# Output projection of a cross-attention block: one float32 product against three float32r products of high and low parts

## What is computed

```python
attn = attn.reshape(b, n, N_HEADS * HEAD_DIM)
return attn @ Wout + bout
...
x = x + _L0_xattn_ref(_layernorm(x, axis=-1), ctx_1024, ...)
x = x + _L0_ffn_ref(_layernorm(x, axis=-1), L0_ffn_w_fc, L0_ffn_w_proj)
```

## Time and profile before

| | us |
|---|---|
| median of 3 runs | 822.95 |
| lowest and highest run | 822.5, 823.52 |
| the profiled execution, its own time | 822.28 |
| its span in the trace | 820.2 |
| PE busy | 778.4 |
| DVE busy | 682.1 |
| ACT busy | 451.8 |
| POOL busy | 337.5 |

### The profile page before, as it was taken

How to read it: one execution, slowest core, us unless ns; L and a number is a source line. 1 busy time by engine, 2 the same in 40 slices (tenths; PEclk the granted TensorE clock), 3 DMA queues, 4 the chain that set the end, 5 groups by cost and what they waited for, 6 DMA issues and landing times.

```text
span 820.2 us, 11697 instructions
## 1 busy us (share of the span) xinstructions
PE 778.4 (95%) x3842; PEld 331.7 (40%) x3842; DVE 682.1 (83%) x937; ACT 451.8 (55%) x825; POOL 337.5 (41%) x428
## 2 busy tenths in 40 slices
PE   1899989799999999999999999899999999999996
PEld 0688877132222222222222222234444444444442
DVE  5988876978888888888888888369999999988983
ACT  4566666177777777777777777744322432233230
POOL 2777867654345544554455545323221211111000
PEclk9999999599999999999999999999999999999998
DMA  8278887734455566675556663226456645553463
GB/s 275 91 204 229 260 231 182 168 92 137 124 140 157 144 138 155 143 162 162 141 150 176 172 162 102 65 61 142 103 116 145 126 90 110 111 127 78 79 127 90
DMA packets 175627, 116.14 MB, mean 142 GB/s; under 512 B 116560, under 2 KB 147280, under 8 KB 175568
## 3 DMA queue, kind: packets, MB, share of 16 engines
q1 hardware_dynamic: 175568, 115.40, 57.6%
HBM read 64.50 MB, written 25.43 MB: 110 GB/s over the span
## 4 chain that ended last, share of the span: by engine, by line
PE 82%; DVE 7%; DMA 3%; ACT 3%; issue 2%; SPq 1%; POOL 1%; DVEq 0%; ACTq 0%; POOLq 0%
PE banks L638 15%; PE banks L625 15%; PE banks L599 13%; PE banks L871 11%; PE banks L883 10%; PE banks L256 8%; PE banks L857 7%; PE banks L280 1%; DVE h_scales L951 1%; DMA stack_words<-max_rows 1%; DVE maxima L669 1%; DVE h_stats L938 1%; ACT probs_words L689 1%; ACT probs_words L1001 1%; DMA probs_words<-in_L_xattn_Wkv_dram 1%
## 5 line engine op out<-in xcount | busy, mean ns | idle before, releaser
L669 DVE TENSOR_REDUCE maxima<-banks 128x2 f32<-128x1024 f32 x256 | 301.8, 1216 | 50.2 <-PE banks L599 50.2
L689 ACT ACTIVATE probs_words<-banks 128x512 f32<-128x512 f32 x512 | 276.0, 597 | 99.9 <-PE banks L625 98.2
L625 PE MATMUL banks<-stack_words 98*128 98x512 bf16 x512 | 175.0, 385 | 2.9 <-ACT probs_words L689 1.8
L599 PE MATMUL banks<-stack_words 96*128 96x512 bf16 x512 | 158.9, 392 | 5.2 <-DVE maxima L669 4.6
L638 PE MATMUL banks<-probs_words,late_words 128*32 128x512 f32 x1024 | 136.4, 605 | 0.5
L883 PE MATMUL banks<-ternary_words,stack_words 128*128 128x512 f16 x512 | 115.3, 384 | 4.5 <-DMA stack_words<-stack_words 4.5
L871 PE MATMUL banks<-ternary_words,late_words 128*128 128x512 f16 x512 | 113.1, 379 | 0.0
L1001 ACT ACTIVATE probs_words<-probs_words,h_moments 128x2048 f32<-128x2048 f32 x16 | 32.0, 2002 | 136.8 <-DVE h_moments L943 136.8
L625 PEld LDWEIGHTS banks<-stack_words 98*128 98x128 bf16 x512 | 39.4, 97 | 143.6 <-ACT probs_words L689 85.1
L703 POOL TENSOR_SCALAR neg_max<-maxima 128x16 f32<-128x16 f32 x32 | 8.3, 258 | 173.4 <-DVE maxima L669 173.4
L883 PEld LDWEIGHTS banks<-ternary_words,stack_words 128*128 128x128 f16 x512 | 50.6, 99 | 70.6 <-issue 14.3
(11 more groups left out here) (127 smaller groups left out, 935.4 us busy)
## 6 DMA issues: line engine op xcount, KB each, us to landing
o_rows<-late_words SPq DMA_DIRECT2D x32, 256.0 KB, 2.7
k_parts<-ternary_words SPq DMA_DIRECT2D x48, 128.0 KB, 2.9
q_parts<-ternary_words SPq DMA_DIRECT2D x48, 128.0 KB, 2.5
stack_words<-q_parts SPq DMA_DIRECT2D x32, 192.0 KB, 3.0
stack_words<-k_parts SPq DMA_DIRECT2D x96, 64.0 KB, 2.7
stack_words<-k_parts SPq DMA_DIRECT2D x32, 192.0 KB, 2.8
attn_words<-in_x_dram SPq DMA_DIRECT2D x16, 256.0 KB, 4.4
probs_words<-in_L_ffn_w_fc_dram SPq DMA_DIRECT2D x16, 256.0 KB, 4.1
```

The source lines that it names most:

```text
L599: mm = self.nc.tensor.matmul(self.score_slot[j % 2][:, i], self.mem.q_stack[0:STACK, slot, head, c * P:(c + 1) * P], self.mem.k_stack[0:ST ...
L625: self.nc.tensor.matmul(self.mem.banks[:, self.ST_BANK[k]], self.mem.k_stack[0:STACK + 2, slot, head, c * P:(c + 1) * P], self.mem.q_stack ...
L669: dve.tensor_reduce(self.maxima[:, g % 2, 2 * j:2 * j + 2], self.score_slot[j % 2], AX.X, ALU.max).then_inc(self.scores_read, 1)
L689: act.activation(self.probs[:, c, head, :], self.mem.banks[:, self.ST_BANK[k]], ACT.Exp, scale=1 / math.sqrt(HEAD)).then_inc(self.exp_done, 1)
```

## The change

`Wout` and each tile of `attnT` are split into a high part, rounded to float32r, and a low part, the rest. `mix` then issues 12 float32r matmuls (high by high, attention high by weight low, attention low by weight high) in place of 4 float32 ones. The new work around it:

- DVE: `weight_high` (two copies of 128x1024) and `weight_low` (two subtractions of 128x1024), once, around the copy of the sums of group 29.
- ACT: `mix_high`, one copy of 128x512 for each of the 16 tiles: for tiles 0 and 1 inside the exponentials of two late attention steps, for tile 2 right after the first `centre_u`, for tile 3 after the second, for later ones after the `centre_u` of their iteration.
- POOL: `mix_low`, one subtraction of 128x512 for each tile: for tiles 0 and 1 in the last attention steps, for tile 2 after `spread_u` of tile 1, for tile 3 after `add_bias` of tile 3, for later ones straight after `add_bias` of the same tile.
- `mix` of tile n now waits for `mix_low` of tile n.
- The parts have memory of their own under v; raw `Wout` is loaded into a slot of the attention stacks, at a later place of SP's queue, x into the buffers of the raw ternary weights, and some other buffers move.

```diff
--- before.py
+++ after.py
@@ -84,6 +84,11 @@
         self.gammas = sb("gammas", [P, 2], F32)
         self.limits = sb("limits", [P, 2, 2], F32)
         self.half_power = sb("half_power", [P, 1], F32)
+        with ExitStack() as early:
+            self.wout_parts = [early.enter_context(nc.sbuf_tensor(f"wout_{part}", [P, KX, DIM], F32R))[:]
+                               for part in ("high", "low")]
+            self.mixT = [early.enter_context(nc.sbuf_tensor(f"mixT_{part}", [P, 2, KX, P], F32R))[:]
+                         for part in ("high", "low")]
         self.v_words = sb("v_words", [P, GROUPS * CHUNKS * GW], F32)
         self.v_all = self.v_words[:].rearrange("p (g c e) -> p g c e", c=CHUNKS, e=GW)
         with ExitStack() as early:
@@ -467,9 +472,9 @@
         self.inverse = slots(late.take(2 * SEQ), 2)
         self.v_ones = late.take(2 * CHUNKS * GH * 2 * HEAD).rearrange("p (s c h e) -> p s c h e", s=2, c=CHUNKS, h=GH)
         self.raw = slots(late.take(2 * DIM), 2)
-        self.below = late.take(DIM // 2, F16)
         self.ternary = slots(late.take(DIM, F16), 2)
         self.late = late
+        self.below = mem.late_words[:, 22 * DIM - DIM // 2:22 * DIM].bitcast(F16)
         self.sums = sb("sums", [P, 2, SUMS], F32)
         self.maxima = sb("maxima", [P, 2, GH * CHUNKS], F32)
         self.neg_max = sb("neg_max", [P, 2, GH * CHUNKS], F32)
@@ -741,17 +746,19 @@
         self.nc, self.mem, self.att = nc, mem, att
         sb, late, banks = mem.sb, att.late, mem.banks
         blocks = lambda words, n: words.rearrange("p (k d) -> p k d", k=n)
-        self.x1 = [late.take(DIM) for i in range(X1_SLOTS - 1)]
+        self.x1 = [late.take(DIM) for i in range(X1_SLOTS - 1)] + [att.ternary.rearrange("p s c -> p (s c)").bitcast(F32)]
         self.u_parts = late.take(2 * DIM, F16).rearrange("p (s t c) -> p s t c", s=2, t=2)
         self.uT = late.take(U_SLOTS * DIM, F16).rearrange("p (s i r) -> p s i r", s=U_SLOTS, r=P)
+        self.bout_sb = late.take(DIM)
+        self.u = mem.late_words[:, 21 * DIM:22 * DIM]
+        self.x_in = att.raw
+        self.wout_raw = [mem.stack_words[:, i * half:i * half + 2 * DIM].rearrange("p (k d) -> p k d", k=2)
+                         for half in (STACK_SLOTS * GH * SEQ // 2,) for i in range(2)]
+        self.wout_parts, self.mixT = mem.wout_parts, mem.mixT
         values = Region(mem.v_words)
-        self.wout_sb = blocks(values.take(KX * DIM), KX)
-        self.bout_sb = values.take(DIM)
-        self.x_in = blocks(values.take(2 * DIM), 2)
+        values.take((KX + 2) * 2 * DIM)
         self.centred = blocks(values.take(2 * DIM), 2)
-        self.u = values.take(DIM)
         self.y = blocks(values.take(2 * DIM), 2)
-        self.x1.append(values.take(DIM))
         self.h = mem.probs_words[:].rearrange("p (s c) -> p s c", s=H_SLOTS)
         stacks = Region(mem.stack_words)
         self.h_parts = stacks.take(2 * FFN, F16).rearrange("p (s t c) -> p s t c", s=2, t=2)
@@ -778,6 +785,10 @@
         self.h_turned = [[sem(f"h_turned_{slot}_{part}") for part in range(2)] for slot in range(2)]
         self.out_stored = [sem(f"out_stored_{i}") for i in range(2)]
         self.wout_loaded = sem("rows_wout_loaded")
+        self.wout_high = sem("rows_wout_high")
+        self.wout_low = sem("rows_wout_low")
+        self.mixT_high = sem("rows_mixT_high")
+        self.mixT_low = sem("rows_mixT_low")
         self.bout_loaded = sem("rows_bout_loaded")
         self.x_bias_ready = sem("rows_x_bias_ready")
         self.mix_ready = sem("rows_mix_ready")
@@ -810,15 +821,16 @@
 
 
     def load_bias(self, sp, bout):
-        sp.wait_ge(self.att.v_staged, 3 * HG)
         sp.dma_start(self.bout_sb, bout.rearrange("(a d) -> a d", a=1).to_broadcast([P, DIM])
                      ).then_inc(self.bout_loaded, DMA)
 
     def load_weight(self, sp, wout, k):
-        sp.wait_ge(self.att.v_staged, 3 * HG)
-        sp.dma_start(self.wout_sb[:, k], wout[k * P:(k + 1) * P]).then_inc(self.wout_loaded, DMA)
+        sp.wait_ge(self.att.st_ready, (GROUPS - STACK_SLOTS + 1) * 16)
+        sp.dma_start(self.wout_raw[k // 2][:, k % 2], wout[k * P:(k + 1) * P]).then_inc(self.wout_loaded, DMA)
 
     def load_x(self, sp, x, n):
+        if n < 2:
+            sp.wait_ge(self.att.ternary_ready, GROUPS - 1 + n)
         need(sp, self.x1_ready, n - 1)
         sp.dma_start(self.x_in[:, n % 2], x.rearrange("b (c p) d -> (b c) p d", p=P)[n]
                      ).then_inc(self.x_in_loaded[n % 2], DMA)
@@ -846,16 +858,15 @@
 
 
     def mix(self, pe, n):
-        att = self.att
-        pe.wait_ge(att.divided, (n // CHUNKS + 1) * KX)
+        pe.wait_ge(self.mixT_low, n + 1)
         if n == 0:
-            pe.wait_ge(self.wout_loaded, KX * DMA)
-            pe.wait_ge(att.scores_read, GROUPS * 2 * GH)
+            pe.wait_ge(self.wout_low, 2)
+            pe.wait_ge(self.att.scores_read, GROUPS * 2 * GH)
         need(pe, self.x1_ready, n - 1)
-        c = n % CHUNKS
-        for k in range(KX):
-            mm = self.nc.tensor.matmul(self.y_bank[n % 2], att.attnT[:, n // CHUNKS * KX + k, c * P:(c + 1) * P],
-                                       self.wout_sb[:, k, :], start=(k == 0), stop=(k == KX - 1))
+        for a, b in ((0, 0), (0, 1), (1, 0)):
+            for k in range(KX):
+                mm = self.nc.tensor.matmul(self.y_bank[n % 2], self.mixT[a][:, n % 2, k], self.wout_parts[b][:, k, :],
+                                           start=(a + b + k == 0), stop=(a == 1 and k == KX - 1))
         mm.then_inc(self.mix_ready, 1)
 
     def expand(self, pe, n, o):
@@ -886,11 +897,24 @@
 
 
 
+    def weight_high(self, dve):
+        dve.wait_ge(self.wout_loaded, KX * DMA)
+        dve.wait_ge(self.att.v_staged, 3 * HG)
+        for i in range(2):
+            dve.tensor_copy(self.wout_parts[0][:, 2 * i:2 * i + 2], self.wout_raw[i]).then_inc(self.wout_high, 1)
+
+    def weight_low(self, dve):
+        for i in range(2):
+            dve.wait_ge(self.wout_high, i + 1)
+            dve.tensor_tensor(self.wout_parts[1][:, 2 * i:2 * i + 2], self.wout_raw[i],
+                              self.wout_parts[0][:, 2 * i:2 * i + 2].bitcast(F32), ALU.subtract).then_inc(self.wout_low, 1)
+
     def add_residual(self, dve, n):
         dve.wait_ge(self.mix_ready, n + 1)
         dve.wait_ge(self.x_bias_ready, n + 1)
         if n == X1_SLOTS - 1:
-            dve.wait_ge(self.att.v_staged, GROUPS)
+            for i in range(2):
+                dve.wait_ge(self.att.wT_turned[i], GROUPS // 2 * DMA)
         need(dve, self.y_ready, n - X1_SLOTS + 1)
         dve.tensor_tensor(self.x1[n % X1_SLOTS], self.y_bank[n % 2], self.x_in[:, n % 2], ALU.add
                           ).then_inc(self.x1_ready, 1)
@@ -916,6 +940,8 @@
         dve.scalar_tensor_tensor(now(3), now(1), 0.0, self.u_powers[:, r, 1:2], ALU.mult, ALU.add
                                  ).then_inc(self.u_step, 1)
         need(dve, self.u_ready, n)
+        if n == 0:
+            dve.wait_ge(self.att.ternary_ready, GROUPS)
         dve.wait_ge(self.u_step, n * 4 + 4)
         dve.tensor_scalar(self.u, self.centred[:, r], now(2), Q_B, ALU.mult, ALU.min).then_inc(self.u_clipped, 1)
         need(dve, self.fc_ready, (n - U_SLOTS + 1) * QUARTERS)
@@ -981,7 +1007,19 @@
 
 
 
+    def turned_rows(self, n):
+        return self.att.attnT[:, n // CHUNKS * KX:(n // CHUNKS + 1) * KX, n % CHUNKS * P:(n % CHUNKS + 1) * P]
+
+    def mix_high(self, act, n):
+        if n == 0:
+            act.wait_ge(self.att.v_staged, 3 * HG)
+        act.wait_ge(self.att.divided, (n // CHUNKS + 1) * KX)
+        need(act, self.mix_ready, n - 1)
+        act.copy(self.mixT[0][:, n % 2], self.turned_rows(n)).then_inc(self.mixT_high, 1)
+
     def centre_u(self, act, n):
+        if n == 0:
+            act.wait_ge(self.att.v_staged, GROUPS)
         act.wait_ge(self.u_stats_ready, n + 1)
         need(act, self.u_clipped, n - 1)
         act.activation(self.centred[:, n % 2], self.x1[n % X1_SLOTS], ACT.Identity,
@@ -1006,6 +1044,12 @@
     def add_bias(self, pool, n):
         pool.wait_ge(self.x_in_loaded[n % 2], (n // 2 + 1) * DMA)
         pool.tensor_tensor(self.x_in[:, n % 2], self.x_in[:, n % 2], self.bout_sb, ALU.add).then_inc(self.x_bias_ready, 1)
+
+    def mix_low(self, pool, n):
+        pool.wait_ge(self.mixT_high, n + 1)
+        need(pool, self.mix_ready, n - 1)
+        pool.tensor_tensor(self.mixT[1][:, n % 2], self.turned_rows(n), self.mixT[0][:, n % 2].bitcast(F32), ALU.subtract
+                           ).then_inc(self.mixT_low, 1)
 
     def spread_u(self, pool, n):
         r = n % 2
@@ -1072,10 +1116,11 @@
                     att.turn_weight(sp, s - 2)
                 if s == GROUPS - 7:
                     rows.load_bias(sp, bout)
-                if GROUPS - 6 <= s < GROUPS - 2:
-                    rows.load_weight(sp, wout, s - GROUPS + 6)
-                if GROUPS - 2 <= s < GROUPS:
```

(19 more changed lines are left out.)

## The result

The changed kernel takes 826.51 us in the median of 7 runs (825.06 to 829.4), the kernel before on the same chips 822.5 (820.2 to 823.89): a ratio of 1.0051, 95% interval 1.0034 to 1.0069. It is slower, by about 4 us. The forecast was 827.6 in a range of 817 to 833. The profiled execution has a span of 823.4 us where the one of before had 820.2.

What follows compares the result with a forecast made beforehand. PE bound the rows stage, DVE 7.6 us under it. DVE's chain, -0.2 start, +1.5 handoff, +11.0 mix_low, -7.65 waits used up, gives +4.65 on 822.95: 827.6 us, range 817 to 833.

Steps and rivals of the forecast that it cites:

- The mixes: On PE, 12 float32r matmuls take 2.85 us against 3.43 for four float32 ones: 0.58 less for a tile.
- PE's own chain: PE's path through the rows stage: -0.2 start, +2.9 handoff, -8.1 for fourteen mixes, in all -5.4 us.
- The eleven mix_low, +11.0: POOL's mix_low of tiles 5 to 15 holds DVE instructions, usually L960 behind add_bias: 1.0 us each, +11.0.
- a mean near 2.2: Sign that the forecast is right: DVE's L960 (later L986) has a mean near 2.2 us instead of 1.29.
- The rule of the Trainium skill: POOL and DVE instructions sharing SBUF ports block each other fully; at its word, eleven mix_low cost 13.5, forecast 830.0.
- Tile 4's at no cost: mix_low of tile 4 on POOL, at 551.65 us beside DVE's four statistics, was taken to cost 0.
- The handoff, +1.5: Around 542 to 546 us, added POOL instructions hold DVE's quantise_u of tile 1: +1.5 on DVE; PE stands still 2.9.
- the start, -0.2: Start of DVE's chain: mixes 0 and 1 -0.6 each, copy on ACT +0.6, copy of sums +0.4: -0.2 us.
- The weight parts on DVE: weight_high's two copies take 1.4 us ahead of group 29's sums, 0.4 later for PE; the subtractions end before mix 0.
- Rival (a): POOL's clash with DVE costs little and PE stays the bound: 817.6 us with c below 0.2; chance 0.20.
- Rival (c): POOL's subtraction with a float32r result takes twice 1.27 us, c near 2.2: end +20, 843 us; chance 0.06.
- Rival (d): float32r gains nothing, 0.86 us a matmul: 6.9 more a mix, some 90 us in all; chance 0.01.

Runs made afterwards that it cites:

- x4_eight: Changed kernel without the third product (attention low by weight high), 4 of 12 matmuls in each mix: 823.46 us, ratio 1.0005 to the kernel before.
- x1: Changed kernel without mix_low on POOL for tiles 4 to 15, the products using a stale low part: 816.84 us, ratio 0.9918 to the kernel before.
- x2: Changed kernel with a second, unused POOL subtraction of the same size ahead of mix_low for tiles 4 to 15: 836.93 us, ratio 1.0171 to the kernel before.
- x3: Changed kernel with, from tile 4 on, mix_high at the start of ACT's iteration and mix_low between spread_h and spread_u: 816.92 us, ratio 0.9929.
- x10: Kernel before plus an unused POOL subtraction of two different 128x512 blocks behind add_bias of tiles 4 to 15: 824.9 us, ratio 1.0032.

## Why the prediction was right, point by point

- **The bound moves from PE to DVE.** Right: shown by the chain, by the waits that are gone, and by x4_eight, where less work on PE left the rounds as they were.
- **The mixes.** 0.58 us less was forecast for a tile; PE's period is shorter by 0.67. Read as rows 3 were, from start to start, a mix takes 2.94 us, not the 2.85 of that row, but the expand ahead of it takes 0.19 less than before. It did not matter, as DVE is the bound.
- **PE's own chain.** Forecast was DVE at +4.65 and PE at -5.4, so 10.05 between them at tile 10. Measured are +3.98 and -6.1 (748.64 against 754.7), 10.1 between them.
- **The eleven mix_low, +11.0.** The twelve rounds grew from 198.2, less 6.0 of waits, to 202.1: 9.9 us, or 0.90 each instead of 1.0. The placement was right to the instruction: L986 in the usual iteration. Its price was 0.97 (2.26 less 1.29), not 1.05: 1.17 us were left of mix_low when L986 came, and L986 was longer by 0.2 less than that. The sign "a mean near 2.2" did not come: the mean of L986 is 1.93, as in four of twelve iterations it is free: in three the forecast itself had put the meeting elsewhere, and the fourth has no mix_low. Summed by line over the twelve rounds, L986 has 7.7 us more, L949 2.8 and L946 1.0; L992 has 1.0 less, since the one that add_bias held in rows 6 is free now. Meetings of other POOL instructions shifted too, so 0.90 is the net price of one more. x1, x2, x3 and x10 show the term from four sides: taken out, doubled, moved, and put into the other kernel. Removed or moved it gives 10 us, added it costs 10.4 in the changed kernel and 9.6 of DVE's time in the kernel before.
- **The rule of the Trainium skill, blocked for the whole instruction,** would have made it 13.5 (and the median 830.1, where the forecast wrote 830.0); the measured 9.9 is nearer to the rows. The meetings do block; but a waiting DVE instruction comes out 0.1 to 0.2 us shorter than wait plus duration (L940 0.13, L986 0.20).
- **Tile 4's at no cost.** Wrong: at 550 us add_bias met the one-column L940 (1.18 us), and mix_low L949 (1.23 us), where before only L930 was held: about 1 us more. It is part of the handoff's size below.
- **The handoff, +1.5, and the start, -0.2.** The first L964 comes at 553.92 instead of 552.12: +1.8 where +1.3 was forecast. That this fits is luck. From the residual of tile 1 to the first L964 it is 15.8 us instead of 12.4, +3.4 where +1.5 was forecast: 1.3 for the held instructions of tile 1, 1.0 for the wait for the mix of tile 2, which ran at a granted clock of 0.62 and was not foreseen, and 1.1 for tile 4. Against it, this execution was already 1.4 us ahead at the start of the attention stage (140.0 us against 141.4). The change does not touch what lies ahead of that, and other executions of either kernel begin the stage between 139.9 and 144.1. From there to the residual of tile 1 it is -0.2, the start as forecast. The stand of PE was forecast at 2.9 and is 2.88.
- **The weight parts on DVE.** Forecast at 1.4 us for the two copies and 0.4 on PE. mix_high takes 0.61 us on ACT, where 0.62 was forecast. In the timeline at 513 us:

```profile
513.01 1.29 DVE L904 CAST wout_high<-stack_words 128x1024 fp32r<-128x1024 f32 x2
...
514.21 0.68 DVE L685 COPY late_words<-banks 128x512 f32<-128x512 f32 x1
...
515.04 1.07 PE L643 MATMUL banks<-probs_words,late_words 128*32 128x512 f32 x8 [0.22 <-DVE late_words L685]
```

The copies take 1.29 in all and PE waits 0.22. The mix of tile 0 found both parts ready.
- **Rival (a), the clash costs little,** is out for this placement, but x1 and x3 measure what it would have given: 816.8 and 816.9, forecast 817.6. **Rival (c),** a dearer subtraction with that result type, is out: 1.29 us in the mean, as add_bias. **Rival (d)** is out with the 2.75 us.
- **The sum.** At `finish` of tile 10 the forecast had +4.65; it is 758.70 against 754.72, +3.98, with the 1.4 us of luck in it. The end is 0.7 less again, because the last contract took 8.77 us in this execution and 9.39 in the one of before. The medians, which do not hang on one pair of executions, differ by 4.0 us, and by their interval by 3 to 6.

## What to carry to other kernels

An instruction put on an idle engine was not free here: look in the timeline at what DVE does at the moment when POOL will run it, and place it beside reductions, statistics and reads of PSUM; ten microseconds lay between two places in the same loop. When the bound engine gets less work, read first how far under it the next one lies (here 7.65 us in 210), and charge every addition against that distance. A probe must have the size of what it stands for: one of 1.04 us in place of 1.27 left the time as it was.

## What the runs showed of the hardware that was not expected

- A DVE instruction of one column was held as long as a wide one: L949 took 1.23 us instead of 0.21 beside a mix_low, L940 1.18 instead of 0.15 beside an add_bias. Both read two tensors.
- In x2_two_lows the instruction that waited went next: after a POOL instruction had held L987, the third POOL instruction took 2.25 us itself. It held DVE all the same: three in a row lengthened L984 by 0.42, L987 by 0.96 and L989 by 1.01 us.
- A POOL subtraction of 128x512 that reads one block twice took 1.04 us, with two different blocks 1.27.
- Twelve float32r matmuls of 128x512, from start to start, took 2.88 us at a granted clock of 1.00, 4.45 at 0.62 and 5.29 at 0.50, each time right after PE had stood for 2.9 us. The same stand was followed by either clock.
